# Second experts: low-rank rows stacked high over low, choice weights by DMA, other order of small work

## The reference

```python
def _fused_linear(x, W, qa, qb, scale, w):
    out = x @ W.T
    a = jnp.einsum('th,krh->tkr', x, qa)
    b = jnp.einsum('tkr,khr->tkh', a, qb)
    mix = jnp.einsum('tkh,tk->th', b, w)
    return out + scale[None, :] * mix
def expert(muW, gW, gqa, gqb, gs, uW, uqa, uqb, us, dW, dqa, dqb, ds, w):
    xe = x + w @ muW.T
    gate = jax.nn.silu(_fused_linear(xe, gW, gqa, gqb, gs, w))
    up = _fused_linear(xe, uW, uqa, uqb, us, w)
    return _fused_linear(gate * up, dW, dqa, dqb, ds, w)
y = jnp.einsum('fth,tf->th', outs, scalar).reshape(b, s, h)
```

## Time and profile before

| what | us |
|---|---|
| median of 3 runs (1079.26 to 1084.4) | 1079.3 |
| the profiled execution's own time | 1087.43 |
| its span | 1085.1 |
| busy in the span: TensorE | 992.0 (91%) |
| VectorE, ScalarE, GpSimd | 720.6, 606.7, 480.1 |

### The profile page before, as it was taken

One profiled execution on the slowest core, in us unless ns is written; L12 is line 12 of the kernel. 1 busy time (PEld: TensorE's weight loads), 2 busy tenths in 40 slices (PEclk: granted clock), 3 DMA queues, 4 the chain that ended last, 5 costly groups with the idle time before them and its releaser, 6 DMA issues. The chain is left out here.

```text
span 1085.1 us, 19309 instructions
## 1 busy us (share of the span) xinstructions
PE 992.0 (91%) x6228; PEld 822.2 (76%) x6228; DVE 720.6 (66%) x2139; ACT 606.7 (56%) x1647; POOL 480.1 (44%) x479
## 2 busy tenths in 40 slices
PE   7999999998996799849999999988878889999996
PEld 5998899887883689827888898975435568777785
DVE  5666766664587356528586757646787457888876
ACT  3656665666222355437676777637774565555553
POOL 5787668762277344354443220211237214443321
PEclk9999999999998799959999999989998999999999
DMA  6732110000011699735312121187003011112101
GB/s 216 255 122 80 30 31 27 18 15 2 1 59 56 186 345 337 258 98 180 97 60 68 50 69 40 59 135 95 21 2 118 0 59 59 59 62 78 38 1 40
DMA packets 86667, 95.60 MB, mean 88 GB/s; under 512 B 8897, under 2 KB 76295, under 8 KB 86576
## 3 DMA queue, kind: packets, MB, share of 16 engines
q1 hardware_dynamic: 82464, 85.48, 26.2%
q0 software_dynamic: 3264, 7.42, 2.2%
q10 hardware_dynamic: 848, 1.57, 0.4%
HBM read 71.22 MB, written 24.12 MB: 88 GB/s over the span
## 5 line engine op out<-in xcount | busy, mean ns | idle before, releaser
L579 POOL TENSOR_TENSOR a_qk<-h,a_by_sin 128x512 f32<-128x512 f32 x64 | 81.9, 1280 | 5.0
L278 PE MATMUL a_mix_ps<-a_probsT,a_v 128*128 128x256 f32 x256 | 78.5, 388 | 5.6 <-ACT a_probsT L310 5.6
L352 DVE CUSTOM_DVE_ANT_0 h<-a_score_ps,mask_bf 128x128 f32<-128x128 f32 (+1 forms) x128 | 40.6, 355 | 58.5 <-PE a_score_ps L345 50.3
L1298 POOL TENSOR_TENSOR a_w_l<-a_w,a_w_h 128x512 fp32r<-128x512 f32 x30 | 38.9, 1296 | 83.3 <-ACT a_w_h L1473 83.3
L358 ACT ACTIVATE y_moe<-y_moe,a_nmax 128x128 f32<-128x128 f32 x64 | 25.6, 400 | 75.8 <-DVE a_nmax L352 75.8
L339 DVE COPY a_probsT<-a_turn_ps 128x384 f32<-128x384 f32 x64 | 34.9, 546 | 48.2 <-PE a_turn_ps L269 48.2
L1025 POOL TENSOR_TENSOR e_w_l<-e_w,e_w_h 128x512 fp32r<-128x512 f32 x32 | 40.8, 1276 | 56.0 <-ACT e_w_h L1093 56.0
L459 PEld LDWEIGHTS a_proj_ps<-a_w,xT 128*128 128x128 f32 x512 | 59.6, 192 | 0.9
L80 PE MATMUL a_proj_ps<-a_x_l,a_w_h 128*128 128x512 f32 x128 | 56.8, 444 | 3.4 <-POOL a_w_l L584 3.3
L459 PE MATMUL a_proj_ps<-a_w,xT 128*128 128x128 f32 x512 | 59.7, 275 | 0.0
L2658 POOL TENSOR_TENSOR m_up_l<-m_up_w,m_up_h 128x1024 fp32r<-128x1024 f32 x8 | 19.4, 2429 | 88.8 <-ACT m_up_h L2630 88.8
(11 more groups left out here) (451 smaller groups left out, 3511.8 us busy)
## 6 DMA issues: line engine op xcount, KB each, us to landing
slots<-zeros SPq DMA_DIRECT2D x4, 2048.0 KB, 8.0
e_rows<-slots SPq DMA_DIRECT2D x32, 256.0 KB, 4.6
e_w<-in_L_ffn_w_dram SPq DMA_DIRECT2D x32, 256.0 KB, 4.8
out_slots<-e_out SPq DMA_DIRECT2D x32, 256.0 KB, 4.1
a_w<-in_L_attn_w_q_dram SPq DMA_DIRECT2D x32, 256.0 KB
e_w<-in_L_ffn_w_dram SPq DMA_DIRECT2D x32, 128.0 KB, 4.2
keys<-key_parts SPq DMA_DIRECT2D x16, 256.0 KB, 11.2
m_up_w<-in_up_dram SPq DMA_DIRECT2D x8, 512.0 KB, 3.6
```

The costliest lines, as they stand in the source:

```text
L278: pe.matmul(self.mix_ps[:, r, 0:S], v(0), self.probsT[:, r, 0:S], start=True, stop=False, skip_group_check=True)
L352: done = dve.tensor_tensor_reduce(self.probs[:, b, cells], self.score_ps[:, r, cells], self.k.mask_bf[:, cells], -1.0, 3e38, ALU.add, ALU. ...
L579: pool.tensor_tensor(qk[:, par, 0 if what == "q" else 1, half * HALF:(half + 1) * HALF], by_cos[:, r, :], by_sin[:, r2, :], ALU.add).then_ ...
```

## The change

For gate and up the low-rank rows are stacked. Two new tiles hold, for 64 rows of `aw` each, the high parts on one half of the partitions and the low parts on the other (`gate_a`: gate's high on 0 to 63, low on 64 to 127; `up_a` the other way round), and the weights' high parts are copied twice, once to each half (`lora_g`, `lora_u`, by `stack_lora`). One matmul over all 128 rows then gives high by high and high by low. `gate_up_lora` becomes two plus two matmuls for tile 0 of gate and up and three for tile 1, without pairs of 64 rows. The down input's act1 gets its low rows on partitions 64 to 127 of the high tile, so its part is two matmuls instead of three; ScalarE then copies those rows to where `down_out` reads them, before awd's cut overwrites the place.

The choice weights are spread by the matmul for expert 0 alone. For the others the route stage copies the turned choice weights to a spare tile, SP stores them in DRAM eight times (once for each r), and two DMAs per step bring 64 rows each into `wrep`. The load of expert e+1 moves behind the even step's awd, and after expert 0 the load of `rep` and its cut go.

GpSimd takes the low part of up's rows (`up_rest`), VectorE keeps gate's. In GpSimd's order `up_rest` of the even step comes before the expert's scaling, that of the odd step after the map's low part. The four clearing copies go. The weights are stacked by ScalarE in odd steps, ahead of aw's cut (for expert 0 in the route stage, ahead of the last silu).

```diff
+                k.ew.stack_lora(act, 0)
...
+                    for side in range(2):
+                        act.activation(k.soft_rows[side * SIDE:(side + 1) * SIDE, halves(half)],
+                                       soft_ps[side][0:SIDE, :], ACT.Copy).then_inc(rows_kept, 1)
...
+    def stack_lora(self, act, e):
+        act.wait_ge(self.lora_scaled, e + 1)
+        tiles = self.lora_s[:, :].rearrange("p (j f) -> p j f", j=GU)
+        for rows in (slice(0, KR), slice(KR, P)):
+            act.activation(self.lora_g[rows, e % 2], tiles[0:KR, 0:GU:2, :], ACT.Copy)
+            act.activation(self.lora_u[rows, e % 2], tiles[KR:P, 1:GU, :], ACT.Copy).then_inc(self.lora_stacked, 1)
...
-                for e in range(2, F1):
-                    ew.load(sp, e)
+                for r in range(R1):
+                    sp.dma_start(k.soft_dram[:, r, :], k.soft_rows).then_inc(rows_stored, 16)
+                sp.wait_ge(rows_stored, 16 * R1)
+                for n in range(2, N):
+                    e, half = divmod(n, 2)
+                    sp.wait_ge(awd_done, n - 1)
+                    rows = k.soft_dram[e * K1:(e + 1) * K1, :, half * HALF:(half + 1) * HALF].rearrange("j r t -> (j r) t")
+                    for again in range(2):
+                        sp.dma_start(wrep[again * KR:(again + 1) * KR, half, :], rows).then_inc(wrep_in[half], 16)
+                    if half == 0 and e + 1 < F1:
+                        ew.load(sp, e + 1)
...
+                def up_rest(n):
+                    pool.wait_ge(aw_high, n + 1)
+                    at_least(pool, gu_done, 2 * n)
+                    pool.tensor_tensor(up_a[0:KR, :], aw[KR:P, :], aw_h[KR:P, :], ALU.subtract).then_inc(up_low, 1)
+                    pool.wait_ge(up_low, n + 1)
                 pool.memset(act1[:, :], 0.0).then_inc(cleared, 1)
+                pool.wait_ge(cleared, 1)
+                up_rest(0)
                 for e in range(1, F1):
+                    if e > 1:
+                        pool.wait_ge(ew.down_low, 2 * e)
+                        up_rest(2 * e - 2)
                     ew.scale(pool, e)
                     ew.cut_mu_low(pool, e)
+                    up_rest(2 * e - 1)
                     ew.cut_up_low(pool, e)
                     ew.cut_lora_low(pool, e)
                     ew.cut_dqa_low(pool, e)
                     ew.cut_down_low(pool, e)
+                pool.wait_ge(ew.down_low, 2 * F1)
+                up_rest(N - 2)
+                up_rest(N - 1)
                 for t in range(0, NT, 2):
...
-                    pe.matmul(a_ps[:, :], rep[:, e % 2, :], soft, start=True, stop=True
-                              ).then_inc(wrep_proj, 1)
+                    if e == 0:
+                        pe.matmul(a_ps[:, :], rep[:, :], soft, start=True, stop=True).then_inc(wrep_proj, 1)
...
-                    pe.wait_ge(aw_low, n + 1)
+                        pe.wait_ge(ew.lora_stacked, 2 * (n // 2) + 2)
+                    pe.wait_ge(aw_stacked, n + 1)
+                    pe.wait_ge(gate_low, n + 1)
+                    pe.wait_ge(up_low, n + 1)
                     e = n // 2 % 2
-                    for left, right in ((lora.h, aw_p.l), (lora.h, aw_p.h), (lora.l, aw_p.h)):
-                        for j in range(2):
-                            rows = slice(j * KR, (j + 1) * KR)
-                            last = pe.matmul(gu_ps[:, j, :], left[rows, e, j * P:(j + 1) * P], right[rows, :],
-                                             start=False, stop=left is lora.l, tile_position=(j * KR, 0))
+                    for j, (left, right) in enumerate(((ew.lora_g, gate_a), (ew.lora_u, up_a))):
+                        pe.matmul(gu_ps[:, j, :], left[:, e, 0, :], right[:, :], start=False, stop=False)
+                        last = pe.matmul(gu_ps[:, j, :], lora.l[:, e, j * P:(j + 1) * P], right[:, :], start=False, stop=True)
                     last.then_inc(gu_done, 1)
-                    product(pe, gu_ps[:, 2, :], lora[:, e, 2 * P:3 * P], aw_p[:, :], False, True).then_inc(gu_done, 1)
...
+                    pe.matmul(gu_ps[:, 2, :], ew.lora_g[:, e, 1, :], gate_a[:, :], start=False, stop=False)
+                    pe.matmul(gu_ps[:, 2, :], ew.lora_u[:, e, 1, :], up_a[:, :], start=False, stop=False)
+                    pe.matmul(gu_ps[:, 2, :], lora.l[:, e, 2 * P:3 * P], aw_h[:, :], start=False, stop=True
+                              ).then_inc(gu_done, 1)
...
-                    if n == 0:
-                        pe.wait_ge(clear_h, 2)
                     if n % 2 == 0:
                         pe.wait_ge(ew.dqa_low, n // 2 + 1)
-                    for c, a in enumerate((act0_p, act1_p)):
-                        pe.wait_ge(act_low, 2 * n + c + 1)
-                        last = product(pe, xe_ps[:, 0, :], dqa[:, n // 2 % 2, c, :], a[:, n % 2, :], c == 0, c == 1)
-                    last.then_inc(dqa_done, 1)
+                    pe.wait_ge(act_low, 2 * n + 1)
+                    product(pe, xe_ps[:, 0, :], dqa[:, n // 2 % 2, 0, :], act0_p[:, n % 2, :], True, False)
+                    pe.wait_ge(act_low, 2 * n + 2)
+                    high, low = dqa[:, n // 2 % 2, 1, :]
+                    pe.matmul(xe_ps[:, 0, :], high, act1_p.h[:, n % 2, :], start=False, stop=False)
+                    pe.matmul(xe_ps[:, 0, :], low, act1_p.h[:, n % 2, :], start=False, stop=True).then_inc(dqa_done, 1)
...
-                    act.activation(aw_p.h[:, :], aw[:, :], ACT.Copy).then_inc(aw_high, 1)
+                    act.activation(aw_h[:, :], aw[:, :], ACT.Copy).then_inc(aw_high, 1)
+                    act.activation(gate_a[0:KR, :], aw[0:KR, :], ACT.Copy)
+                    act.activation(up_a[KR:P, :], aw[KR:P, :], ACT.Copy).then_inc(aw_stacked, 1)
...
-                act.wait_ge(cleared, 1)
-                for r in range(2):
-                    act.activation(act1_p.h[KR:P, r, :], act1[KR:P, :], ACT.Copy)
-                    act.activation(act1_p.l[KR:P, r, :], act1[KR:P, :], ACT.Copy).then_inc(clear_h, 1)
...
+                    if n % 2 and n // 2 + 1 < F1:
+                        ew.stack_lora(act, n // 2 + 1)
                     if n + 1 < N:
                         keep_aw(n + 1)
+                    act.wait_ge(act_low, 2 * n + 2)
+                    act.activation(act1_p.l[0:KR, n % 2, :], act1_p.h[KR:P, n % 2, :], ACT.Copy
+                                   ).then_inc(rest_kept, 1)
+                    act.wait_ge(rest_kept, n + 1)
                     act.wait_ge(awd_done, n + 1)
                     act.activation(act1_p.h[KR:P, n % 2, :], act1[KR:P, :], ACT.Copy).then_inc(awd_high, 1)
                     if n + 2 < N:
...
                     dve.wait_ge(a_proj, n + 1)
+                    if n >= 2:
+                        dve.wait_ge(wrep_in[n % 2], 16 * 2 * (n // 2))
+                    at_least(dve, up_low, n)
+                    at_least(dve, aw_stacked, n)
                     dve.tensor_tensor(aw[:, :], a_ps[:, :], wrep[:, n % 2, :], ALU.mult).then_inc(aw_done, 1)
...
-                    dve.tensor_tensor(aw_p.l[:, :], aw[:, :], aw_p.h[:, :], ALU.subtract).then_inc(aw_low, 1)
+                    dve.tensor_tensor(gate_a[KR:P, :], aw[0:KR, :], aw_h[0:KR, :], ALU.subtract).then_inc(gate_low, 1)
...
-                    dve.tensor_tensor(act1_p.l[0:KR, n % 2, :], act1[0:KR, :], act1_p.h[0:KR, n % 2, :], ALU.subtract
+                    dve.tensor_tensor(act1_p.h[KR:P, n % 2, :], act1[0:KR, :], act1_p.h[0:KR, n % 2, :], ALU.subtract
                                       ).then_inc(act_low, 1)
```

More of the change, by code:

```diff
@@ L2217, in layer1_route @@
         soft_low = m.sem("s_soft_low")
+        rows_kept = m.sem("s_rows_kept")
         soft_turned = m.sem("s_soft_turned")
@@ L2557 @@
 AT = GU * P
-LOADS1 = 8
+LOADS1 = 7
 class ExpertWeights:
@@ L2579, in __init__ @@
         self.mu = m.sb("m_mu", [P, 2, D], F32R)
-        self.rep = m.sb("m_rep", [P, 2, P], F32R)
+        self.rep = m.sb("m_rep", [P, P], F32R)
+        self.lora_g = m.at("m_lora_g", [P, 2, 2, P], k.wo1_at + 8 * 4 * D, F32R)
+        self.lora_u = m.at("m_lora_u", [P, 2, 2, P], k.wo1_at + 10 * 4 * D, F32R)
         self.w_in = [m.sem("m_w_in0"), m.sem("m_w_in1")]
         self.ones_in = m.sem("m_ones_in")
+        self.lora_stacked = m.sem("m_lora_stacked")
         self.lora_scaled, self.down_scaled = m.sem("m_lora_scaled"), m.sem("m_down_scaled")
@@ L2623, in cut_mu_high @@
         self.loaded(act, e)
-        act.activation(self.rep[:, r, :], self.rep_w[:, r, :], ACT.Copy)
+        if e == 0:
+            act.activation(self.rep[:, :], self.rep_w[:, :], ACT.Copy)
         act.activation(self.mu[:, r, :], self.mu_w[:, r, :], ACT.Copy).then_inc(self.mu_high, 1)
@@ L2699, in layer1_experts @@
         cleared = m.sem("m_cleared")
-        clear_h = m.sem("m_clear_h")
+        rows_stored = m.sem("m_rows_stored")
+        rest_kept = m.sem("m_rest_kept")
+        wrep_in = [m.sem("m_wrep_in0"), m.sem("m_wrep_in1")]
```

(8 more changed lines are left out.)

23 lines of the change are left out of this document (16 added, 7 removed).

## The result

The changed kernel takes 1090.6 us (median of 7 runs, 1088.54 to 1092.36) against 1082.1 for the kernel before on the same chip (7 runs, 1079.26 to 1084.74): 1.0070 of it, with a 95% interval of 1.0046 to 1.0093. It is slower by 0.7%. The profiled execution took 1089.0, its span is 1087.2.

A forecast was written before the change was run, and what follows sets the result against it. Bound: a VectorE, ScalarE, VectorE chain in one half of an expert, TensorE in the other with 0.18 us to spare. Experts +1.5, start +0.7, end -1.0, route +1.2 sum to +2.4: 1082 us, range 1073 to 1088.

The forecast's parts named there:

- The port in the steady loops: Experts' loops: VectorE keeps the read port in the even one; GpSimd's scaling makes the odd one's L2985 end 1.1 later.
- first rival: Even loop: GpSimd's new subtraction gets the read port before VectorE's L2929; +4.2, in all +6.6, 1085.9; port or waits 0.24.
- second rival: Experts' stage: TensorE's saving comes through, the chain shortening with it; -8.4, 1071; at least half through 0.20.
- copies of 64x512 follow each other at 0.54: ScalarE between the cuts of aw and awd: three new copies at this spacing let L2985 start at +3.63 after aw.
- some 0.4 to 0.5 is left ... I take 0.3: Odd loop: what remains of L2985 ending 1.1 later once slack absorbs the rest; taken as 0.3 per expert.
- Three margins: Odd loop: removed cut of rep some 0.2, ScalarE's idle 0.24 before L2885, and L2925's wait of 0.18 absorb delay.
- the experts' term: Seven experts at -0.09 (even loop) + 0.3 (odd loop) = +0.2 each: +1.5 us.
- The +1.0 for loop 0: Start of the experts' stage: L2985 follows L2925 by 3.63 instead of 2.62, and nothing there absorbs it.
- The 0.3 taken back for the clearing copies: Loop 0: the four clearing copies ahead of the first silu are gone, returning 0.3, so the start costs +0.7.
- The route stage: Four stacking copies of 64x256 at 0.31 make the last silu 1.24 late, and TensorE's last products with it: +1.2.
- The tail: Last two steps: no weights to cut, so they are TensorE's; 2 x 0.40 + 0.23 = -1.0 us.
- Transfers: Choice weights' stores and loads and the later weight loads stay hidden, costing nothing; late transfers as a rival: 0.06.

The follow-up runs named there:

- early copy: Changed kernel with ScalarE's copy of act1's low rows moved ahead of aw's cut: 1086.5 us beside 1082.4 for the kernel before; an expert 10.86 + 14.51 = 25.37.
- The experiment with the scaling first: Changed kernel with GpSimd's scaling of the next expert ahead of its subtraction for the even step: 1086.7 us beside 1081.8 for the kernel before.
- the run with the other order: Changed kernel with the four stacking copies reordered, the two to lora_g first, then the two to lora_u: 1093.6 us beside 1081.8 for the kernel before.

## Why the prediction was wrong in size and right in kind

The predicted 1082.0 was 8.6 below the measured time, which lies above the range (1073 to 1088). Slower by more than 0.5% had been given 0.25. Of the 8.6, 2.8 are the base: the kernel before had 1079.3 in the three runs shown and 1082.1 in the seven of the comparison. The rest is the sum, +2.4 forecast and +8.5 measured. So the chain that bounds an expert was named rightly, and what failed are the sizes put on it: the margin that absorbs the odd loop's delay, the spacing of ScalarE's copies, the route stage, and a term that the sum didn't have. Point by point:

- **The bound.** Right. The chain VectorE, ScalarE, VectorE sets an expert, and TensorE's saving is worth nothing: two matmuls more per step made an expert 0.03 longer, the map's matmul taken back 0.08, and TensorE idles 1.2 us more per expert.
- **The port in the steady loops.** Right, by a hair: VectorE kept it in both by 0.04 us, and the odd loop's low part was stretched to 1.07 under the scaling. The first rival's mechanism (GpSimd gets the port, L2990 over 1.5) did come in loop 0, where it was hidden, and behind the last aw, where no run separates its cost; in the steady even loops only the runs with the early copy have it. The Trainium skill, SBUF — State Buffer, section "Who interferes with whom", has the two engines exclude each other by order of issue; in the steady loops L2781 starts 0.04 after L2990 and loses, in loop 0 it starts 0.03 ahead and wins, and in the early-copy run 0.37 ahead and wins, so the order agrees in these rows. Where the forecast says that by the page's order the second rival is likelier, it is the first that the order bears on.
- **ScalarE's copies.** The step "copies of 64x512 follow each other at 0.54" was mis-sized. That spacing was read from clears with input and output on the same half of the partitions. The new ones alternate between halves and stand 0.63 and 0.65 apart, so awd's low part starts at +3.86 and not at +3.63. The even loop, costed at -0.09, costs +0.14 there and +0.22 in all, 0.11 of it by the next point.
- **The sums behind act1's low part.** No term in the forecast, which moved this instruction's output to the upper half of the partitions at no cost. The sums now start 0.11 later behind it in each loop.
- **What absorbs it.** The step "some 0.4 to 0.5 is left ... I take 0.3" failed. The forecast had awd's low part end 1.1 late in the odd loop. Three margins with a row each were to take back 0.62 of that, and a guess without a row (a waiting instruction may run shorter) another 0.2. The end came 1.18 late, and the time from there to the next aw shrank from 7.48 (rows 4) to 6.92, so that 0.62 was left instead of 0.3. The three margins came nearly as read: VectorE's rows in the odd loop are 1.17 late at xe's low part and 0.75 late at act1's, and from the last sum to aw it is 0.26 less, with the 0.18 named. The guessed 0.2 did not come, and 0.11 was lost again at the sums. The twelve intervals after the first two came to +4.9 where the experts' term said +1.5. This is the largest error, 3.4 us.
- **The start.** +1.7 for +0.7. The +1.0 for loop 0 is the second interval: awd's low part came 1.25 later instead of 1.01, and the interval is 1.36 longer (1.2 by the copies alone). The 0.3 taken back for the clearing copies did not come: the silu there starts 6.2 after aw in both kernels, since it now waits 1.69 us for TensorE, and the first interval is 0.3 longer.
- **The route stage.** +3.06 for +1.2: the copies are 0.43 apart and not 0.31 (1.7), and TensorE has the low clock for longer in its last matmuls, another 1.15. The forecast had no term for the clock, though the kernel before already has it at 0.50 for 3.4 us of this very stretch. That the longer wait is what prolonged it is likely and not shown.
- **The tail.** -0.5 for -1.0. The forecast took the last two steps to be TensorE's alone; no run separates what else has a part.
- **Transfers.** Right: never waited for.

The 0.84 of an expert divides so. ScalarE's three copies, added alone to the kernel before, cost 0.30. The rest, 0.44 in the odd loop and 0.10 in the even one, is read by comparing the changed kernel's rows with that run's: in the odd loop L3046 lasts 0.38 longer under GpSimd's scaling, 0.06 of which is taken up before the next silu, and the sums behind act1's low part start 0.11 later in each loop. So the port costs about 0.32 and the sums 0.22. The experiment with the scaling first agrees: it brings 0.28 back and leaves 0.11 of the stretch in place.

Two things lay outside what the forecast named: TensorE's clock in the route stage, and the spacing behind act1's low part. Four terms were too small, all with the same sign: experts 3.4, route 1.9, start 1.0, tail 0.5, together 6.8 (less 0.15 at the stage's start), more than the 6 that the range allowed above the forecast.

## What to carry to other kernels

When an engine is 99% busy, ask first what it waits for in each loop: if a chain of three small operations on other engines ends last, work taken from the busy engine is worth nothing, and what is put into that chain is paid as soon as its small slack is used up. Take the price of a copy from a row with the same places of input and output, not only the same size; an output that moves to other partitions has its price too, on the instruction behind it. Count the margins that a row shows, and none that is guessed: here the three that were read came, and the guessed one didn't. Two engines that share a port have to be ordered for the whole loop: each wait that freed one operation here moved the meeting to the next one.

## What the runs showed of the hardware

- ScalarE's copies on 64 partitions: 0.53 to 0.54 apart for 512 columns where the two have the same input half and output half, 0.63 where both halves change and 0.65 where the output's does. For 256 columns it is 0.31 on all partitions, 0.41 and 0.43 on 64 where only the input's half changes (the changed kernel) or only the output's (the run with the other order), and 0.44 where both do.
- VectorE's sums into y start 0.61 after a 64x512 subtraction of 0.68 that writes to partitions 0 to 63, and 0.72 after one that writes to 64 to 127, with the same inputs (all ten kernels with the new place, the two without it).
- The same 24 matmuls lasted 6.87 to 8.45 us, with TensorE's clock at 0.50 (1.2 GHz) for 2.9 to 6.1 us of it and at full speed (2.4 GHz) for the rest; duration times granted clock is 5.4 us in all twelve profiles.
- Whole executions of one kernel differ with the mean granted clock: 17 runs of the kernel before on one chip have clocks from 0.956 to 0.969, with 1090.1 us at 0.956 and 1079.7 to 1080.5 at 0.969 in four of them. A difference of a few us between single executions has to be read from stretches of the trace.
- A 64x512 subtraction with two SBUF inputs lasted 0.69, 1.04 to 1.07, 1.47 or 1.82 on VectorE, and 1.28 or 1.80 on GpSimd. Which it was followed from 0.03 to 0.4 us of order between the engines; in the even loop with the early copy that order was worth 0.4 us an expert.
